# A DLRM tower on one core: products with 26 stationary features per sample, last layers in four column groups, stores per chunk, closing stage in another order

## What is computed

```python
e = jnp.stack([tbl_0[ids[:, 0]], ..., tbl_25[ids[:, 25]]], axis=1)      # 2048 x 26 x 128
sd = jnp.einsum('bfd,bd->bf', e, dense)                                  # 26 products with the dense row
ss = jnp.einsum('bfd,bgd->bfg', e, e)
pairs = ss[:, iu, ju]                                                    # the 325 with f < g
h = jnp.concatenate([dense, sd, pairs, dense], axis=1)                   # 607 columns
h = jnp.maximum(h @ W_top1 + b_top1, 0.0)                                # 512
h = jnp.maximum(h @ W_top2 + b_top2, 0.0)                                # 256
y = h @ W_top3                                                           # 1
```

## Time and profile before

| | us |
|---|---|
| median of 3 runs (lowest, highest) | 373.24 (372.98, 373.9) |
| profiled execution | 373.56 |
| its span on the core | 371.8 |
| PE busy, PEld busy | 346.7, 274.4 |
| POOL, DVE, ACT busy | 263.2, 252.6, 176.2 |

### The profile page before, as it was taken

The page is one execution under the profiler, slowest core; times in us unless marked ns, Lnnn a source line. Parts: engine busy times, 40 slices in busy tenths (PEclk is TensorE's granted clock), DMA queues, the critical chain, the costliest instruction groups (busy, mean ns, idle before and its releaser), DMA issues.

```text
span 371.8 us, 13904 instructions
## 1 busy us (share of the span) xinstructions
PE 346.7 (93%) x5585; PEld 274.4 (74%) x5585; DVE 252.6 (68%) x502; ACT 176.2 (47%) x300; POOL 263.2 (71%) x276
## 2 busy tenths in 40 slices
PE   2899997969999999999999999999899999899987
PEld 0566665757778888887778888887678778779876
DVE  1689889938688773678798753877789672445231
ACT  3366578753613323767514325678213335433332
POOL 6777878777777777777777777777777777777200
PEclk9999999996999999999999999999999999969999
DMA  7999214234333332243333222233333122222100
GB/s 183 247 238 231 66 50 100 54 95 116 94 92 86 86 76 83 60 111 95 91 93 104 86 75 71 75 102 89 97 109 88 51 59 56 56 54 55 26 4 0
DMA packets 21170, 33.51 MB, mean 90 GB/s; under 512 B 8628, under 2 KB 11589, under 8 KB 21107
## 3 DMA queue, kind: packets, MB, share of 16 engines
q0 software_dynamic: 8608, 17.65, 18.7%
q1 hardware_dynamic: 12499, 14.98, 15.4%
HBM read 32.60 MB, written 0.01 MB: 88 GB/s over the span
## 4 chain that ended last, share of the span: by engine, by line
PE 38%; POOL 8%; issue 3%; DMA 2%; ACT 1%; DVE 1%; ACTq 0%
POOL rows L606 8%; PE late_bank L725 7%; PE gram_bank L676 5%; PE turn_bank L657 3%; PE late_bank L630 3%; PE late_bank L631 2%; PE spare_bank L772 2%; PE gram_bank L630 2%; PE gram_bank L631 2%; DMA rows<-in_tbl_dram,index 2%; PE spare_bank L630 1%; PE gram_bank L704 1%; PE turn_bank L630 1%; PE turn_bank L631 1%; PE spare_bank L631 1%
## 5 line engine op out<-in xcount | busy, mean ns | idle before, releaser
L606 POOL DMA_INDIRECT rows<-in_tbl_dram,index x269 | 262.4, 976 | 83.0 <-issue 80.1
L1176 DVE TENSOR_TENSOR one_hot<-table_ids,row_number 125x512 fp32r<-125x512 int32 x216 | 134.5, 681 | 32.7 <-PE gram_bank L631 13.0
L418 ACT COPY turned<-turn_bank 128x512 f32<-128x512 f32 (+1 forms) x69 | 68.1, 1030 | 49.6 <-PE turn_bank L657 45.3
L630 PE MATMUL late_bank<-one_hot,table_hi 125*128 125x512 f32 x168 | 72.9, 434 | 5.4 <-DVE one_hot L1176 3.5
L631 PE MATMUL late_bank<-one_hot,table_lo 125*128 125x512 f32 x168 | 68.5, 408 | 0.0
L676 PEld LDWEIGHTS gram_bank<-turned 128*27 128x27 f32 x4096 | 45.8, 106 | 19.7 <-issue 15.5
L676 PE MATMUL gram_bank<-turned 128*27 128x26 f32 x4096 | 55.4, 193 | 3.4 <-DVE turned L432 1.4
L630 PEld LDWEIGHTS late_bank<-one_hot,table_hi 125*128 125x128 f32 x168 | 32.9, 196 | 20.0 <-issue 5.3
L657 PE MATMUL turn_bank<-ident,rows 128*128 128x128 f32 x285 | 43.5, 277 | 4.4 <-DMA rows<-in_tbl_dram,index 2.8
L657 PEld LDWEIGHTS turn_bank<-ident,rows 128*128 128x128 f32 x285 | 34.9, 142 | 13.7 <-DMA rows<-in_tbl_dram,index 4.3
L1174 DVE TENSOR_SCALAR one_hot<-looked_up,row_number_sb 125x512 fp32r<-125x512 f32 x72 | 32.8, 496 | 12.4 <-issue 6.4
(11 more groups left out here) (138 smaller groups left out, 449.1 us busy)
## 6 DMA issues: line engine op xcount, KB each, us to landing
table_ids<-in_ids_by_table_dram SPq DMA_DIRECT2D x27, 256.0 KB, 3.1
fetched<-in_tbl_dram SPq DMA_DIRECT2D x384, 0.5 KB
rows<-in_tbl_dram,index POOLq DMA_INDIRECT x269
turned<-in_tbl_dram SPq DMA_DIRECT2D x6, 448.0 KB, 13.5
looked_up<-in_tbl_dram SPq DMA_DIRECT2D x3, 448.0 KB, 6.0
rows<-in_r_dense_features_dram SPq DMA_DIRECT2D x16, 64.0 KB, 1.8
gram<-in_W_top_dram SPq DMA_DIRECT2D x1, 702.0 KB
gram<-in_W_top_dram SPq DMA_DIRECT2D x1, 512.0 KB
```

Of the source, the lines that this page charges most:

```text
L418: copy(to[:, f0:f1], of).then_inc(rows_copied[n % 2], 1)
L606: pool.indirect_dma_start(out=rows[:, row % RING_ROWS, :], out_offset=None, in_=tables[f], in_offset=bass.IndirectOffsetOnAxis(ap=index[:, ...
L630: pe.matmul(bank, table_hi[:, s, k, :], hot, start=k == 0, stop=False)
L1176: last = nc.vector.tensor_tensor(hot, table_ids[0:RK, (chunk.n * LOOKUPS + s) % ID_SLOTS, 0:wide], row_number[0:RK, k:k + 1].broadcast_to( ...
```

## The change

1. `products` multiplies weights of 26 columns (features 1 to 26) with the same 26 moving columns (features 0 to 25); row i of the result is now feature i + 1, and `copy_cols` reads accordingly. The results take 26 partitions of each group of 32 instead of 27 (ACROSS is 122 for 124).
2. `layer3` now has w3 as weights (one column) and 128 samples as moving columns, one tile in each column group; `half_layer3` splits its 256 samples over the four column groups, 64 each. Results lie on partitions 0, 32, 64, 96.
3. Each chunk's results are stored when they are there, by ACT (`store`); `turn_outputs`, `copy_output_rows` and SP's `store_rows` are gone. They lie in `gram`'s room, so that DVE waits for the store before it copies unit 10 of the next chunk.
4. The closing stage has another order: FINAL's dense part of block 2 and EARLY's layer 3 stand one unit later among the products; FINAL's first block of layer 1 takes the products as their operands become ready; layer 2 of block 0 comes one block later; the last relu is DVE's.

```diff
-ACROSS = (GROUP - 1) * QUAD + QUAD - 4
+ACROSS = (GROUP - 1) * QUAD + LATER
+FINAL_LAYER2_AFTER = ((), (), (0,), (1, 2))
...
-        y_bank = late_bank[0][:, 0:TILES]
-        y_rows_bank = late_bank[1][0:LAST.first, 0:P]
-        last_y_bank = whole_turn_bank[0][0:1]
+        y_bank = late_bank[0][:, 0:P]
+        last_y_bank = whole_turn_bank[0][:, 0:HALF * QUAD]
...
+            if chunk.n > 0 and chunk is not LAST and n == Y_UNIT:
+                engine.wait_ge(stored, chunk.n * DMA)
...
-                last = copy(pairs_of(part)[:, :, offset(i):offset(i + 1)], of[:, :, i + 1:FEATURES])
+                last = copy(pairs_of(part)[:, :, offset(i):offset(i + 1)], of[:, :, i:LATER])
...
-                sp.dma_start(out[part.first * P:(part.first + part.tiles) * P, :].rearrange("b n -> n b"),
-                             last_y[:, samples_of(part)]).then_inc(stored, DMA)
+                sp.dma_start(out[part.first * P:(part.first + part.tiles) * P, :].rearrange("(g b) n -> g (b n)", g=GROUP),
+                             y_quarters[0:P:QUAD, y_of(part)]).then_inc(stored, DMA)
...
-            store_rows()
             store_half(EARLY)
             store_half(FINAL)
-            sp.wait_ge(stored, 3 * DMA)
+            sp.wait_ge(stored, PARTS * DMA)
...
-                        last = pe.matmul(gram_bank[n % 2][q * QUAD:q * QUAD + FEATURES, k * LATER:(k + 1) * LATER],
-                                         sample, sample[:, 0:LATER], start=True, stop=True)
+                        last = pe.matmul(gram_bank[n % 2][q * QUAD:q * QUAD + LATER, k * LATER:(k + 1) * LATER],
+                                         sample[:, 1:FEATURES], sample[:, 0:LATER], start=True, stop=True)
...
-                    if g == 0:
-                        pe.wait_ge(y_rows_copied, 1)
...
+            def final_first_layer1():
+                for k in range(1, K1):
+                    pe.wait_ge(pairs_hi_made, FINAL.n * K_PAIRS + k)
+                    for w in (w1_hi, w1_lo):
+                        pe.matmul(h1_bank(FINAL, 0), w[0:height(k), k, 0:P], input_hi[0:height(k), k, samples_of(FINAL)],
+                                  start=False, stop=False)
+                    if k > 1:
+                        pe.wait_ge(pairs_split, FINAL.n * K_PAIRS + k - 1)
+                        pe.matmul(h1_bank(FINAL, 0), w1_hi[0:PK, k - 1, 0:P], input_lo[0:PK, k - 1, samples_of(FINAL)],
+                                  start=False, stop=False)
+                pe.wait_ge(pairs_split, (FINAL.n + 1) * K_PAIRS)
+                pe.matmul(h1_bank(FINAL, 0), w1_hi[0:PK, K1 - 1, 0:P], input_lo[0:PK, K1 - 1, samples_of(FINAL)],
+                          start=False, stop=True).then_inc(h1_summed, 1)
...
-                for t in range(part.tiles):
-                    for k in range(N2):
-                        last = pe.matmul(y_bank[:, t:t + 1], h2_of(part, k)[:, t * P:(t + 1) * P], w3_sb[:, k:k + 1],
+                for k in range(N2):
+                    for t in range(part.tiles):
+                        last = pe.matmul(y_bank[t * QUAD:t * QUAD + 1], w3_sb[:, k:k + 1], h2_of(part, k)[:, t * P:(t + 1) * P],
                                          start=k == 0, stop=k == N2 - 1)
...
-                    pe.wait_ge(h2_made, (part.n + 1) * N2 + k + 1)
-                    last = pe.matmul(last_y_bank[:, 0:width(part)], w3_sb[:, k:k + 1], h2_of(part, k), start=k == 0, stop=k == N2 - 1)
+                    if part is FINAL and k == 1:
+                        pe.wait_ge(last_h2_made, 1)
+                    else:
+                        pe.wait_ge(h2_made, (part.n + 1) * N2 + k + 1)
+                    for g in range(GROUP):
+                        samples = slice(g * HALF * QUAD, (g + 1) * HALF * QUAD)
+                        last = pe.matmul(last_y_bank[g * QUAD:g * QUAD + 1], w3_sb[:, k:k + 1], h2_of(part, k)[:, samples],
+                                         start=k == 0, stop=k == N2 - 1)
...
-                turn_outputs()
                 products(LAST, 1, 3)
...
                 products(LAST, 3, 0)
+                products(LAST, 3, 1)
                 dense_ahead(FINAL, 2)
-                products(LAST, 3, 1)
+                products(LAST, 3, 2)
                 half_layer3(EARLY)
-                products(LAST, 3, 2)
                 products(LAST, 3, 3)
...
-                for n in range(N1):
+                final_first_layer1()
+                for n in range(1, N1):
                     layer1(FINAL, n)
-                    for k in LAYER2_AFTER[n]:
+                    for k in FINAL_LAYER2_AFTER[n]:
                         layer2(FINAL, k)
...
+            def store(chunk):
+                act.wait_ge(y_copied, chunk.n + 2)
+                act.dma_start(out[chunk.first * P:(chunk.first + TILES) * P, :].rearrange("(t b) n -> t (b n)", t=TILES),
+                              (closing_y_room if chunk is CLOSING else y_room)[0:P:QUAD]).then_inc(stored, DMA)
...
                             copy_output(CHUNKS[chunk.n - 1])
+                            store(CHUNKS[chunk.n - 1])
...
-                for n in range(N2):
-                    relu2(FINAL, n)
+                relu2(FINAL, 0)
                 copy_output(FINAL)
...
+                dve.wait_ge(h2_summed, (FINAL.n + 1) * N2)
+                nc.vector.tensor_scalar(h2_of(FINAL, 1), h2_bank(FINAL, 1), b2_sb[:, 1:2], 0.0, ALU.add, ALU.max).then_inc(last_h2_made, 1)
```

31 lines of the change are left out of this document (13 added, 18 removed).

## The result

The changed kernel takes 375.37 us (median of 20 runs, 373.22 to 377.08), the kernel before 373.96 (20 runs, 372.87 to 375.61): ratio 1.0031, 95% interval 1.0018 to 1.0043. By that ratio it is 1.2 us slower; I had predicted 0.9 us faster. (The quotient of the two medians is 1.0038, or 1.4 us, inside the interval.)

A forecast was written before the change was run, and what follows sets the result against it. Gathers on POOL were taken as the clock until 327.39, then PE behind three more gates; terms -0.05 -0.15 +0.18 -0.33 -0.42 -0.15 = -0.92 us take 373.24 to 372.3, range 371.7 to 373.0.

The forecast's parts named there:

- so 1.4 us less, three times, all before 327.39: 0: Chunks' layer 3 in four column groups: PE time saved before 327.39 only lengthens waits for gathers, so 0.
- rival 1: Slower: PE's clock falls in longer waits near 258 and 262, delaying the load at 296.92 and SP's fetches; 374.6, chance 0.13.
- each wait was clearly shorter than the 3.5 us: Argument against a clock fall near 258 and 262: an earlier fall followed a wait from 80.7 to 84.2.
- 0.4 us of slack for the fetches: At the turn of the fetched row near 349: delay decides only above 0.4 + 0.75 + 1.1 us.
- Stores: 0, between -0.1 and +0.2: Last store in four pieces of 256 B for one of 1 KB: 0; ACT's three chunk stores also 0.
- The products: 26 columns of weights for 27: 0.05 us less in all, between 0 and 0.2.
- half_layer3(EARLY) behind the stall: Closing stage: EARLY's layer 3 moved behind PE's 0.88 us instruction stall; +0.18 us, between 0 and +0.3.
- can't pass in less than 3.8 us: Closing stage: a block of some 254 PE instructions needs at least 3.8 us, which causes the 0.88 us stall.
- FINAL's first block: FINAL's first block of layer 1 starts earlier by taking products as operands become ready; -0.33 us, between -0.36 and 0.
- Last layer 3 and copy: End of kernel: relu on DVE and four column groups -0.42 us, ACT's copy of 64 columns for 256 -0.15.
- The turn of outputs and the gates: Dropping the output turn behind 327.39, limited by gates at 347.65 and 349.28; -0.15 us, between 0 and 0.35.
- The rule weighed: Skill's 60 cycles per matmul: 16 passes of split layer 3 cost 0.40 us for the predicted 0.22, giving 372.7.

The follow-up runs named there:

- layer3: Kernel before with only the chunks' layer 3 in four column groups, one store per chunk issued by ACT and no turn of outputs; ratio 1.0033.
- late_fetch: Kernel before with SP starting its last 96 fetches one turn of rows later; ratio 1.0127.
- two_stores_less: The layer3 run without the first two chunks' stores and without DVE's wait for them; ratio 1.0032 to the kernel before.
- before_early: Kernel before with 32 of SP's last 96 fetches issued ahead of the last load of dense rows; ratio 0.9989.

## Why the prediction was wrong

**The step that failed** is "so 1.4 us less, three times, all before 327.39: 0". The 2.8 us that PE saves by 262 don't vanish in the waits for gathers. They lengthen one wait, the clock falls behind it, and what PE does next opens a load that 49.4 us of fetches stand behind. The last of them comes 2.63 us later than before, 0.88 of which the gathers are later too; less the slack of 0.5, the turn starts 1.3 us too late. Over the runs the gate costs the change some 1.0 us. That was rival 1, in its place and in its chain, with 0.13 of the chance; it should have been the forecast. Three things made it likelier than I gave it:

- I put the wait at 262 at 1.5 to 2 us, and one of 2 us at 258; in the trace they are 3.23 and 0.43. The last gather before it ends at 260.94, 0.65 us after SP issued the load of the next ids (260.29), and its turn starts 2.68 later, with the DMA engines 80% busy. In before that load came at 262.20, 2.5 us behind the gather. In the six traces in which the load is 0.3 to 0.7 us ahead of the end of that gather, the turn starts 2.5 to 3.4 us after it, and the clock falls in all six. In the traces where it is level or behind, it is 1.6 to 2.9. PE's own speed had moved the load, since SP issues it when the one-hots of an earlier table are made, and these wait for PE. That the load delays the gather is argued from this ordering; all six traces are of kernels with the whole change or nearly all of it, and no run moved the load alone. The kernel before, with a load behind the gather, also shows 2.7.
- I argued that each wait was clearly shorter than the 3.5 us of the earlier trace rows. The clock fell behind waits of 2.17 us (layer3) and 2.37 (late_fetch, which at this place is the kernel before), and didn't behind 2.14 (two_stores_less).
- I counted 0.4 us of slack for the fetches and a price from 2.25 us of delay up. The slack was right (the gate opens at 347.41 + 1.27 = 348.68, the turn came at 349.17). But I weighed one execution. In others the kernel before may have none either: before_early gains 0.5, at the edge of the noise.

**Stores: 0, between -0.1 and +0.2** was too small. The last one costs 0.45 more inside the span (1.95 to 1.97 from issue to end in four pieces, 1.49 in one), and the time outside grew by 0.4. Both are size errors in a term that I had nearly written off, and together they are about as large as the -0.92, which fits that the change gains nothing where both kernels fetch early. Of the 0.4, two stores or their wait made 0.34 in one run; how the rest adds up stays open, as it sits where no trace looks.

**What held.** The products: 0. half_layer3(EARLY) behind the stall: +0.18 predicted; in the first pair of traces the first closing unit to the first turned pairs is 8.66 us for 8.73, so -0.07. But the stall scatters: with the same instructions on PE, before and before_early differ by 0.43. Over the traces, first closing unit to first turned column is 4.76 to 5.55 us with EARLY's layer 3 ahead of the stall (eight traces) and 5.15 to 5.61 with it behind in four groups (seven), 0.2 more on average, as predicted. The stall is the instructions' by all signs, though no run took it away on purpose: the DMA view of 353 to 355 in the changed kernel has one packet of queue 8, which takes 1.15 us (3.6% of 16 engines in 2 us). It lies in the second closing unit, and the stall ends at 356.22, behind it.

```profile
q8 instruction: 1, 0.02, 3.6%
```

But "can't pass in less than 3.8 us" is wrong: from the first closing unit to the end of the stall it is 3.94 us before, 3.68 after, 3.50 in before_early, 3.41 with layer 3 alone, and in two_stores_less there is no stall in the third unit at all, with the same order of instructions on PE from there on. FINAL's first block: -0.33 predicted, -0.23 measured. Last layer 3 and copy: -0.57 predicted, -0.48 measured, all of it from the four groups and the shorter copy and none from the relu on DVE. The turn of outputs and the gates: -0.15 predicted; swallowed by the gate, not measurable. With the gate opened the span is 0.75 us under before, near my 0.92, but that agreement is luck: 0.5 of it came with the early fetches on the kernel before as well, and the total, outside time included, is 0.0002 above that of before_early.

The rule weighed: EARLY's layer 3 starts at 356.44 and the next unit at 356.66, so its sixteen passes (the row's x16) take 0.22 us of PE's stream, just what I had taken. The Trainium skill, page "TensorEngine Tiling (Array Packing)", section Instruction Overhead, with its 60 cycles for each matmul, would give 0.40, an estimate from that page. The trace does not agree: in four column groups a pass takes 14 ns of the stream and not 25. The rule has no part in the miss.

## What to carry to other kernels

Time that an engine saves ahead of a wait does not simply vanish there: follow what the engine releases behind that wait, above all transfers in another queue, and what its clock does when the wait grows. A long chain of small transfers that starts on a turn's release is a gate with a fixed length, here 52.4 us from turn to turn; start part of it before the release that it doesn't need. One trace's slack is one draw: with spans that scatter by 4 us (371.0 to 374.9), a gate with 0.5 us of slack can bind in some executions. And a kernel that one edit makes 0.8 us shorter is compared with the old kernel under the same edit before the gain is credited to the change.

## What the runs showed of the hardware that I had not expected

- The clock's fall near 325 came in all ten traces with the one-column layer 3 (1.95 us of small matmuls) before the waits, and in four of nine with the new form (0.65 us in the changed kernel's trace). Where it stayed away, as in layer3, PE reached tile 15's third group 1.5 us after its gather for 4.4 before.
- The Trainium skill, page "Runtime: NRT & Kernel Launch", section Instruction fetch mechanics, says that blocks of 256 instructions are fetched ahead and the cost is mostly hidden. The packets show the blocks (16.4 KB each), but where loads and matmuls pass at 10.6 ns a pair PE stood up to 1.65 us, by all signs for one.
- Time outside the span goes with the program: 1.78 to 1.81 us or 2.13 to 2.21 on average, steady within 0.15 from run to run. With the relu on DVE and the chunks' layer 3 as before it was 1.79 to 2.09 in single runs, 1.95 and 1.96 on average. What sets it was not found.
